# Contexts and organ weights turned outside the late stage, and 16 attention tiles turned by VectorE and a DMA round trip

## The chip, the cores and the metric

The kernel runs on one core of a Trainium2 chip. The metric is the device time of one execution in microseconds (us), lower is better. Every duration below comes from one profiled execution of the kernel before.

## What is computed

Two blocks of two layers each, on latents `x` of 16 batches x 64 tokens x 512 and a context `ctx_4096` of the same shape. Cut to what matters:

```python
x = x + L0_xattn(layernorm(x), ctx)      # 32 heads, 8 key/value heads, RMS-normed q and k, kv = [ctx, latents]
x = x + L0_ffn(layernorm(x))             # 4-bit weights (512 x 1376, twice, and 1376 x 512), silu(x Wg) * (x Wu) @ Wd
x = x + L1_xattn(ctx, layernorm(x), ctx) # below
x = x + L1_ffn(layernorm(x))             # x W_org^T + a mixture of 8 rank-64 products, weighted by softmax(mean(x) Wq^T keys^T)

def L1_xattn(k, q, v):                   # each (16, 64, 512); the 512 features are the positions
    scores = einsum('bcn,bcm->bnm', k, q) / sqrt(64)   # 512 x 512 in every batch
    return einsum('bnm,bcm->bcn', softmax(scores, axis=-1), v)
```

## The kernel before, in words

One program, all five engines, ordered by hand: each engine's instructions are written in the order in which it runs them, and semaphores join the engines. Products are made in a split form: a value is cut into a high part (rounded to fp32r, a `Copy` on ScalarE) and a low part (a subtraction on VectorE or GpSimd), and each 512-wide product is two or three matmuls of these parts.

The work comes in three stages:

- **L0 attention**, 64 steps (`run_steps`) of one key/value head and one pair of batches each. The context, turned so that features lie on partitions, stays in `kvT` for all of it. In every step the queries and the probabilities make a round trip through DRAM (`blocks_out`, `blocks_back`, tensors `q_turn` and `p_turn`): VectorE turns 32x32 blocks, one DMA writes them out and another reads them back in an order that finishes the turn of the tile. Beside it the 4-bit weights are unpacked in 35 chunks by `dequant` on VectorE and stored.
- **L0 FFN**, first half of the tokens, then the first three tiles of the second half (`pe_ffn` and its fellows).
- **The late stage** (`pe_slot`, `act_slot`, `dve_slot`, `pool_slot`), 64 *slots* and 8 more to run out. It holds L1 attention, the rest of the L0 FFN and the L1 FFN. Slot k begins with the scores of tile k (a batch has four tiles of 128 positions). What follows in the slots for one tile t: the row maximum (VectorE L1995), exp (ScalarE L1883, into `pr`), the scaling by 1/sum (GpSimd L2125), then the turn of the 128x512 tile by four TensorE transposes into a PSUM bank (`pe_weights`, L1588), its high part (ScalarE L1869) and low part (VectorE L1999) into `pmT`, and the two value products with the turned context `vS` (`pe_values`, L1604). In every slot up to 24 there are also 12 matmuls of the L0 FFN (`pe_piece`: `half_product` L1697 and `down` L1073). From slot 24 on the L1 FFN takes their place by a table `LATE` of (slot, half) to pieces: *base* (3 matmuls, L1715), *rank* (6, L1738), *delta* (3, L1748).

Tile t is turned in slot t + 5 (t + 6 from tile 24 on) and multiplied with the values in slot t + 6 (t + 8). *Extras* are groups of four TensorE transposes that stand between the two halves of a slot's work (`pe_extra`): the context of a pair of batches for `vS` (`pe_context`, L1513, followed by `act_values` and `dve_values`), the new latents x4, and in slots 17 to 21 and 23 the organ weights `W_org`, `Wq` and the keys (L1816, L1774, L1777). SP issues the DMAs of the late stage in a list of its own (`sp_l1x`): `stack` copies the high and low parts of a batch's context and queries (4 DMAs, L1422 and L1423), `context` loads `cx`.

Of the kernel before, what the change touches and what calls it, by code (L numbers as in the profile page):

```python
# [58 lines left out]
def block_kernel(nc, a, out, stop=None):  # L59
# [28 lines left out]
    with root:  # L88
# [104 lines left out]
        wq1 = at(185376, "wq1", [P, D], F32)  # L193
# [18 lines left out]
        keys = at(226784, "keys", [EXP, KD], F32)  # L212
# [668 lines left out]

        def sp_tables(sp, kinds):
# [48 lines left out]
        def sp_stores(sp, j):  # L931
# [145 lines left out]
        def pe_ffn(pe):  # L1077
# [3 lines left out]
            for n in range(FT + ALONE):  # L1081
# [11 lines left out]
                if n == FT + 1:  # L1093
                    pe_context(pe, 0)
# [24 lines left out]
        def x2_hi(act, p):  # L1119
            act.wait_ge(s_tx2, p + 1)  # L1120
# [12 lines left out]
        def act_ffn(act):  # L1133
            for n in range(FT + ALONE):
# [100 lines left out]
        def dve_ffn(dve):  # L1235
            for n in range(FT + ALONE):
# [23 lines left out]
                if n == FT + 1:  # L1260
                    dve_values(dve, 0)
# [31 lines left out]
        def add_down(dve, half):  # L1293
# [22 lines left out]
        (s_wot, s_woh, s_wol, s_sm, s_smc, s_dnh, s_dnl, s_uph, s_upl, s_tx4, s_x4h, s_x4l, s_mean) = (
            sem(f"s_{n}") for n in ("wot", "woh", "wol", "sm", "smc", "dnh", "dnl", "uph", "upl", "tx4", "x4h", "x4l", "mean"))
# [30 lines left out]
        def pr_of(n):  # L1348

            if n >= FAR // KT and n % 3 == 2:  # L1350
                return prw, 0
            return pr, KT * (n % 2 if n < FAR // KT else n % 3)

        def pm_of(t):
            return t % 2 if t < FAR else t % 3

        def x_bank(k):
            return bank[3] if k < WIDE else bank[6]

        def context_slot(q):  # L1360
            return PT_ * q - 2 if PT_ * q <= FAR else PT_ * q + 5

        def x4_slot(p):
            return sum_slot(2 * p + 1) + (2 if sum_slot(2 * p + 1) < WIDE else 3)
# [11 lines left out]
        def extra_evicted(pe, k):  # L1376

            kind, n = EXTRA[k]
            if kind == "context":
                pe.wait_ge(s_vTl, n + 1)  # L1380
            elif kind == "x4":
                pe.wait_ge(s_x4l, n + 1)
                pe.wait_ge(s_mean, n + 1)
            elif kind == "worg":
                pe.wait_ge(s_wol, n + 1)
            elif kind == "wq":
                pe.wait_ge(s_smc, 1)
            elif kind == "keys":
                pe.wait_ge(s_smc, 2)
# [835 lines left out]
```

## Time and profile before

| | |
|---|---|
| median of 3 runs | 1080.45 us (1080.32 to 1084.87) |
| the profiled execution | 1080.24 us, its span 1078.4 us |
| TensorE busy | 1038.6 us, 96% of the span |
| VectorE, ScalarE, GpSimd busy | 66%, 50%, 44% |
| mean granted TensorE clock | 0.995 |

The span runs from the first to the last instruction, and 1.84 us of the execution lie outside it. TensorE's busy share includes matmuls that overlap, so the length of a slot on TensorE, from one tile's scores to the next one's, is what prices are read from here.

### The profile page before, as it was taken

To read this page: it belongs to the slowest core of one execution; us is meant where nothing else is said; L and a number is where in the kernel's file an instruction comes from. 1 tells how busy PE (TensorE), PEld (TensorE's weight loads), DVE (VectorE), ACT (ScalarE), POOL (GpSimd) and SP (SyncE) were. 2 spreads that over 40 slices of the span, in tenths; PEclk is the share of its full clock that TensorE was granted. 3 is DMA by queue.
4 is the path that set the end of the run, shared out by engine and by line. 5 is a ranking of instruction groups with operands and counts; after the bars stand their busy time and mean duration, and the time that the engine had idled before them with its cause. 6 is when DMAs were issued, how large, how long until landed. Compare 5 with 4: busy or idle time off the path is not lost. (4 is left out here: it accounts for less than half of the span.)

```text
span 1078.4 us, 18680 instructions
## 1 busy us (share of the span) xinstructions
PE 1038.6 (96%) x6021; PEld 897.1 (83%) x6021; DVE 711.7 (66%) x1435; ACT 536.8 (50%) x1974; POOL 469.5 (44%) x446
## 2 busy tenths in 40 slices
PE   5899999999999999999999999899999999899998
PEld 5789999999899899899999998778777877677877
DVE  6677767667666667667676666653345666889862
ACT  3555555555555555555555454433324445456531
POOL 3445454565554554554645433300013325566521
PEclk9999999999999999999999999999999999899999
DMA  8447766676667666766666435242021344233301
GB/s 284 112 130 226 207 192 198 195 206 196 199 198 195 201 192 186 214 204 201 210 191 187 145 99 167 98 136 82 1 59 40 79 108 108 69 69 69 89 11 40
DMA packets 151397, 156.18 MB, mean 145 GB/s; under 512 B 19640, under 2 KB 104656, under 8 KB 151300
## 3 DMA queue, kind: packets, MB, share of 16 engines
q1 hardware_dynamic: 146804, 138.08, 44.0%
q0 software_dynamic: 4496, 16.91, 5.3%
q8 instruction: 49, 0.80, 0.3%
q14 instruction: 48, 0.39, 0.1%
HBM read 98.19 MB, written 44.30 MB: 132 GB/s over the span
## 5 line engine op out<-in xcount | busy, mean ns | idle before, releaser
L459 PEld LDWEIGHTS bank<-wqkv,kvT 128*128 128x128 f32 x1536 | 193.9, 193 | 8.2 <-issue 3.6
L439 PE MATMUL bank<-wqkv,kvT 128*128 128x512 f32 x768 | 195.4, 404 | 5.0 <-DVE wqkv L746 2.5
L459 PE MATMUL bank<-wqkv,kvT 128*128 128x256 f32 x1536 | 196.2, 285 | 3.0 <-issue 3.0
L800 POOL TENSOR_TENSOR rms<-msq,half_neg 128x4 f32<-128x4 f32 x64 | 79.5, 1242 | 270.0 <-DVE msq L703 270.0
L505 PE MATMUL bank<-wo,aoT 128*128 128x512 f32 x768 | 190.7, 398 | 0.3 <-DVE aoT L659 0.3
L439 PEld LDWEIGHTS bank<-wqkv,kvT 128*128 128x128 f32 x768 | 141.2, 191 | 34.1 <-issue 3.2
L505 PEld LDWEIGHTS bank<-wo,aoT 128*128 128x128 f32 x768 | 139.8, 189 | 26.4 <-DVE aoT L659 0.5
L606 ACT ACTIVATE prob<-bank,nmax 128x128 f32<-128x128 f32 x256 | 90.4, 365 | 56.4 <-DVE nmax L674 56.4
L646 ACT ACTIVATE aoT<-bank 128x512 fp32r<-128x512 f32 x64 | 38.2, 597 | 121.7 <-PE bank L526 96.2
L803 POOL TENSOR_TENSOR pT<-pR,pT 128x512 fp32r<-128x512 f32 x64 | 82.3, 1286 | 14.4 <-ACT pT L595 14.4
L613 ACT ACTIVATE qB<-bank 128x128 f32<-128x128 f32 x256 | 67.3, 278 | 39.7 <-PE bank L439 36.2
L711 DVE TENSOR_TENSOR bank<-bank,rms 128x512 f32<-128x512 f32 x64 | 44.8, 699 | 55.8 <-POOL rms L800 55.8
L1054 PE MATMUL bank<-x2T,wgu 128*128 128x512 f32 (+1 forms) x336 | 80.9, 396 | 0.4 <-DVE wgu L1015 0.4
L2125 POOL TENSOR_TENSOR pr<-pr,rc 128x512 f32<-128x512 f32 x52 | 54.4, 1048 | 54.5 <-DVE rc L1989 54.3
L674 DVE TENSOR_REDUCE nmax<-bank 128x4 f32<-128x512 f32 x64 | 44.2, 691 | 50.1 <-PE bank L469 50.0
L1054 PEld LDWEIGHTS bank<-x2T,wgu 128*128 128x128 f32 (+1 forms) x336 | 62.4, 187 | 15.9 <-DVE wgu L1015 0.8
L626 ACT ACTIVATE kT<-bank,wqk 128x256 f32<-128x256 f32 x64 | 30.6, 478 | 87.9 <-PE bank L485 87.9
L469 PE MATMUL bank<-kT,qT 128*128 128x128 f32 x512 | 67.8, 275 | 2.0 <-DMA qT<-q_turn 1.3
L1073 PE MATMUL bank<-wd,hT 128*128 128x512 f32 (+1 forms) x264 | 65.5, 396 | 0.0
L469 PEld LDWEIGHTS bank<-kT,qT 128*128 128x128 f32 x512 | 62.8, 192 | 2.5 <-DMA qT<-q_turn 1.5
L723 DVE TENSOR_TENSOR kn<-bank,rms 128x256 f32<-128x256 f32 x64 | 27.2, 425 | 52.0 <-POOL rms L808 52.0
L1869 ACT ACTIVATE pmT<-bank 128x512 fp32r<-128x512 f32 x64 | 38.2, 596 | 46.4 <-PE bank L1588 46.2
(176 smaller groups left out, 2021.4 us busy)
## 6 DMA issues: line engine op xcount, KB each, us to landing
q_turn<-qB SPq DMA_DIRECT2D x64, 256.0 KB
qT<-q_turn SPq DMA_DIRECT2D x64, 256.0 KB, 3.6
p_turn<-pB SPq DMA_DIRECT2D x64, 256.0 KB, 2.1
pR<-p_turn SPq DMA_DIRECT2D x64, 256.0 KB
qS<-qhl SPq DMA_DIRECT2D x32, 256.0 KB, 3.7
wqkv_raw<-in_L_xattn_Wq_dram SPq DMA_DIRECT2D x30, 256.0 KB
wo_raw<-in_L_xattn_Wo_dram SPq DMA_DIRECT2D x30, 256.0 KB
wload<-w_gu SPq DMA_DIRECT2D x20, 256.0 KB, 3.2
```

Of the source, the lines that this page charges most:

```text
L439: mm = pe.matmul(b_q[:, :], kvT[:, l, kt, p, 1:3, :], wqkv[:, par, r, kt, 0:QW], start=(kt == 0 and n == 0), stop=(kt == KT - 1 and n == 2))
L459: mm = pe.matmul(kv_bank(st, 0)[:, b * 256:(b + 1) * 256], kvT[:, l, kt, p, 2 * b:2 * b + 2, :], wqkv[:, par, r, kt, QW:QKV], start=(kt == ...
L469: mm = pe.matmul(b_s[:, n * P:(n + 1) * P], qT[:, n, :, :], kT[:, n // 2, :], start=True, stop=True)
L505: mm = pe.matmul(b_o[:, :], aoT[:, l, h, :, :], wo[:, par, r, h, :], start=(h == 0 and n == 0), stop=(h == G - 1 and n == 2))
L606: act.activation(prob[:, :, n, :], b_s[:, n * P:(n + 1) * P].rearrange("p (k b) -> p b k", b=4), ACT.Exp, bias=nmax[:, n:n + 1], accum_out ...
L613: act.activation(qB[:, h, :, :], b_q[:, h * HD:(h + 1) * HD], ACT.Square, accum_out=ssq[:, h:h + 1]).then_inc(s_qsq, 1)
L711: dve.tensor_tensor(b_n[:, :].rearrange("p (b h d) -> p b h d", b=4, h=G), b_q[:, :].rearrange("p (h d b) -> p b h d", h=G, b=4), rms[:, 0 ...
L800: pool.tensor_tensor(rms[:, 0:4], msq[:, 0:4], half_neg[:, 0:4], ALU.pow).then_inc(s_rq, 1)
L803: pool.tensor_tensor(pT[:, LO, :, :, :], pR[:, :, :, :], pT[:, HI, :, :, :].bitcast(F32), ALU.subtract).then_inc(s_plo, 1)
L1054: mm = pe.matmul(b[0:w, :], wgu[:, f, l, m, kt, 0:w], x2T[:, r, kt, :], start=(kt == 0 and k == 0), stop=(kt == KT - 1 and k == 2))
L1073: mm = pe.matmul(f_d[t][:, :], hT[0:w, l, t * P:(t + 1) * P], wd[0:w, f, r, :], start=(f == 0 and k == 0), stop=(f == FT - 1 and k == 2))
L2125: pool.tensor_tensor(of[:, to + t % KT, :], of[:, to + t % KT, :], rc1[:, t % 4:t % 4 + 1].to_broadcast([P, D]), ALU.mult).then_inc(s_n1, 1)
```

## The change

- **Contexts.** In steps 24 to 31 of L0 attention SP stores the turned contexts, high and low parts, from `kvT` to a DRAM tensor `ctx_turned` (`context_store`, four DMAs of 128 KB a step in runs of 256 bytes). In the late stage `vS` of a pair is one DMA load (`values`), and `pe_context`, `act_values` and `dve_values` are gone.
- **Organ weights and Wq.** In step 59 SP loads them into buffers of the unpacking, which has ended (`late_raw`), VectorE turns their 32x32 blocks in steps 60 to 62 (`late_turn`, five instructions), and SP stores them in steps 61 to 63 (`late_store`, 20 DMAs in runs of 128 bytes). In the late stage they are loaded already turned; their high parts are made on ScalarE from SBUF (`organ_hi`) and the low parts on GpSimd. The keys are loaded turned, by elements.
- **Tiles 0 to 15** (`TURN` = 16, four groups of four). exp writes its columns in another order; VectorE turns 32x32 blocks (`turn_tile`, 16 instructions), four DMAs write the group out (`turn_out`), four bring it back tile by tile (`turn_back`) into two landing places. The high part is taken in slot t + 7 from SBUF, the low part in the next slot, and the value products follow in slot t + 8. Tiles from 16 on are turned by TensorE in slot t + 7 up to tile 24 and t + 6 after that, all with values at t + 8.
- **The table LATE** is moved to fit: x4 of the first pairs comes 2 or 3 slots later, and so do the first rank pieces (from slot 34 instead of 32).

The core of the diff:

```diff
+        def context_store(sp, p):
+            sp.wait_ge(s_chi, PAIRS)
+            sp.wait_ge(s_clo, PAIRS - 1)
+            for to, (part, b) in enumerate(((HI, 0), (LO, 0), (LO, 1), (HI, 1))):
+                sp.dma_start(ctx_turned[p, :, :, to, :], kvT[:, part, :, p, 3 * b, :].bitcast(F32)).then_inc(s_ct_out, 16)
...
         def weights_slot(t):
-            return t + 5 if t < FAR else t + 6
+            return t + 7 if t <= FAR else t + 6
         def values_slot(t):
-            return t + 6 if t < FAR else t + 8
+            return t + 8
...
-        EXTRA = {**{context_slot(q): ("context", q) for q in range(1, PAIRS)},
-                 **{x4_slot(p): ("x4", p) for p in range(PAIRS - 1)},
-                 **{17 + i: ("worg", i) for i in range(KT)}, 21: ("wq", 0), 23: ("keys", 0)}
+        EXTRA = {x4_slot(p): p for p in range(PAIRS - 1)}
...
+            def turn_out(n):
+                sp.wait_ge(s_pB, UNITS + KT * (n + 1))
+                for m in range(KT):
+                    sp.dma_start(l_turn[n][m].rearrange("s u r -> (s u r)").rearrange("(p c) -> p c", p=P),
+                                 lB[:, m, :, :, :].rearrange("p b c j -> p (b c j)")).then_inc(s_p_out, 16)
+            def turn_back(t):
+                n, m = divmod(t, KT)
+                sp.wait_ge(s_p_out, outs(KT * (n + 1)))
+                if t >= 2:
+                    sp.wait_ge(s_p1l, t - 1)
+                sp.dma_start(lR[:, t % 2, :].rearrange("p (s r) -> p s r", s=G),
+                             l_turn[n][m].rearrange("s u r -> u s r")).then_inc(s_p_back2[t % 2], 16)
...
+            for n in range(B):
+                if n < TURN // KT:
+                    turn_out(n)
+                    turn_back(KT * n)
+                    turn_back(KT * n + 1)
+                    if n == 2:
+                        organ_loads()
+                    if n == 3:
+                        down_loads()
+                    turn_back(KT * n + 2)
...
+                if n + 3 < B:
+                    stack(n + 3)
...
+                if n < TURN // KT:
+                    turn_back(KT * n + 3)
...
         LATE = {
-            (24, 0): (("base", 0, 0),),
-            (25, 0): (("base", 0, 1),),
+            (24, 0): (("base", 0, 0), ("base", 0, 1)),
...
-            (32, 1): (("rank", 0, 0), ("rank", 0, 1),),
+            (34, 1): (("rank", 0, 0), ("rank", 0, 1),),
...
+            if k in TURNED_AT:
+                t = TURNED_AT[k]
+                act.wait_ge(s_p_back2[t % 2], backs(t))
+                if t >= 2:
+                    act.wait_ge(s_v1, t - 1)
+                act.activation(turned(HI, t), landed(t), ACT.Copy).then_inc(s_p1, 1)
...
+        def turn_tile(dve, t):
+            dve.wait_ge(s_n1, t + 1)
+            if t % KT == 0 and t >= KT:
+                dve.wait_ge(s_p_out, outs(t))
+            dve.transpose(lB[:, :, :, t % KT, :].rearrange("p m b j -> p (m b) j"),
+                          pr[:, t % KT, :].rearrange("p (k j) -> p k j", j=32)).then_inc(s_pB, 1)
```

**TensorE, slots 16 and 17.** Before (`ident` marks a transpose, `qS,kS` the scores that open a slot, `pmT,vS` the values that close it, `x2T,wgu` and `wd,hT` the FFN):

```order
L1568 MATMUL bank<-qS,kS 128x512 x2
L1588 MATMUL bank<-ident,pr 128x128 x4
L1073 MATMUL bank<-wd,hT 128x512 x6
L1822 MATMUL bank<-ident,xn 128x128 x4
L1073 MATMUL bank<-wd,hT 128x512 x6
L1604 MATMUL bank<-pmT,vS 128x512 x2
L1568 MATMUL bank<-qS,kS 128x512 x2
L1588 MATMUL bank<-ident,pr 128x128 x4
L1697 MATMUL bank<-x2T,wgu 128x512 x6
L1816 MATMUL bank<-ident,worg 128x128 x4
L1697 MATMUL bank<-x2T,wgu 128x512 x6
L1604 MATMUL bank<-pmT,vS 128x512 x2
```

The same two slots in the changed kernel:

```order
L1643 MATMUL bank<-qS,kS 128x512 x2
L1117 MATMUL bank<-wd,hT 128x512 x12
L1679 MATMUL bank<-pmT,vS 128x512 x2
L1643 MATMUL bank<-qS,kS 128x512 x2
L1771 MATMUL bank<-x2T,wgu 128x512 x12
L1679 MATMUL bank<-pmT,vS 128x512 x2
```

All 16 transposes of the two slots are gone (those of x4 stand in slot 19), and each run of 12 FFN matmuls is whole.

**VectorE, slots 15 and 16 of the changed kernel** (`nm` is the row maximum that opens a slot, `pmT<-pmT` the low part of a turned tile, `STREAM_TRANSPOSE` the block turn, `rc` the reciprocal of a row sum):

```order
L2058 TENSOR_REDUCE nm<-bank 128x1
L2062 TENSOR_TENSOR pmT<-pmT 128x4x4x32
L1334 TENSOR_TENSOR hT<-hval,hT 128x512
L2101 STREAM_TRANSPOSE pr<-pr 128x16x32 x2
L1320 SCALAR_TENSOR_TENSOR gact<-gact,bank 128x512
L2052 RECIPROCAL rc<-sm 128x1
L2058 TENSOR_REDUCE nm<-bank 128x1
L2062 TENSOR_TENSOR pmT<-pmT 128x4x4x32
L2122 TENSOR_TENSOR acc<-bank,acc 64x512
L2124 TENSOR_TENSOR acc<-bank,acc 64x512
L2101 STREAM_TRANSPOSE pr<-pr 128x16x32
```

Three block turns are new here, and the low part now reads its tile from SBUF instead of from a PSUM bank.

**SP, the third group (tiles 8 to 11) of the changed kernel:**

```order
L1483 DMA l_turn<-pr 128x512 x4
L1491 DMA pmT<-l_turn 128x4x128 x2
L1503 DMA worg<-organ_turned 128x4x512
L1491 DMA pmT<-l_turn 128x4x128
L1477 DMA kS<-chl 64x512
L1478 DMA qS<-qhl 64x1024
L1477 DMA kS<-chl 64x512
L1478 DMA qS<-qhl 64x1024
L1464 DMA vS<-ctx_turned 128x1024
L1491 DMA pmT<-l_turn 128x4x128
```

Before, SP's list held here only the stack, the context load and the loads of the organ weights; eight DMAs a group and one load of `vS` a pair are new.

## Rows read from the trace of the kernel before

**Rows 1.** The page, part 1: busy us (share of the span) xinstructions

```profile
PE 1038.6 (96%) x6021; PEld 897.1 (83%) x6021; DVE 711.7 (66%) x1435; ACT 536.8 (50%) x1974; POOL 469.5 (44%) x446
```

**Rows 2.** Windows of the late stage: slots 0-4, 5-7, 8-18, 19-24, 25-33, 34-41, rest

```profile
core 0: us, PE busy (x) PEld busy (x) DVE busy (x) ACT busy (x) POOL busy (x), PEclk, DMA share, GB/s
809.00:825.80 16.80, 16.43 (x71) 13.02 (x70) 9.05 (x19) 8.67 (x17) 6.89 (x8) 1.00 0.00 0
825.80:839.05 13.25, 13.04 (x63) 10.11 (x63) 6.93 (x14) 5.63 (x12) 4.62 (x5) 1.00 0.51 116
839.05:889.16 50.11, 49.21 (x238) 38.58 (x236) 33.97 (x65) 21.98 (x47) 14.96 (x17) 1.00 0.40 91
889.16:919.09 29.93, 29.45 (x146) 22.04 (x144) 19.18 (x38) 16.20 (x34) 15.22 (x14) 1.00 0.39 98
919.09:946.70 27.61, 22.64 (x117) 17.34 (x115) 22.66 (x49) 14.82 (x38) 16.67 (x18) 0.88 0.29 68
946.70:967.29 20.59, 19.29 (x113) 15.33 (x111) 17.95 (x39) 12.26 (x29) 14.68 (x17) 1.00 0.40 90
967.29:1078.40 111.11, 102.24 (x596) 84.27 (x596) 76.44 (x164) 45.89 (x111) 42.27 (x49) 1.00 0.20 51
```

**Rows 3.** Timeline of TensorE: starts of slots 2, 3, 8, 9, 17, 18, one value product

```profile
815.46 0.62 PE L1568 MATMUL bank<-qS,kS 128*128 128x512 f32 x2
...
818.71 0.63 PE L1568 MATMUL bank<-qS,kS 128*128 128x512 f32 x2
...
839.05 0.62 PE L1568 MATMUL bank<-qS,kS 128*128 128x512 f32 x2
...
842.75 0.63 PE L1604 MATMUL bank<-pmT,vS 128*128 128x512 f32 x2
843.22 0.63 PE L1568 MATMUL bank<-qS,kS 128*128 128x512 f32 x2
...
878.71 0.63 PE L1568 MATMUL bank<-qS,kS 128*128 128x512 f32 x2
...
883.58 0.64 PE L1568 MATMUL bank<-qS,kS 128*128 128x512 f32 x2
```

**Rows 4.** VectorE by source line: duration ns min/median/max

```profile
L696 DVE STREAM_TRANSPOSE pB<-bank x64: 716/716/717, 38.4 to 684.9; 128x512 f32<-128x512 f32 x64
...
L1288 DVE TENSOR_TENSOR hT<-hval,hT x22: 676/692/1043, 698.6 to 915.5; 128x512 fp32r<-128x512 f32 x20, 96x512 fp32r<-96x512 f32 x2
```

**Rows 5.** DMAs: SP's issue (ns), landing of the page's part 6 (us), of qT

```profile
L372 SPq DMA_DIRECT2D p_turn<-pB x64: 319/332/339, 39.2 to 685.7; - x64
...
L1423 SPq DMA_DIRECT2D qS<-qhl x31: 589/599/1900, 800.6 to 1008.0; - x31
...
p_turn<-pB SPq DMA_DIRECT2D x64, 256.0 KB, 2.1
...
draw<-in_L_ffn_lora_down_dram SPq DMA_DIRECT2D x4, 256.0 KB, 4.4
...
DMA to landing us min/median/max: 2.5/3.6/7.1
```

**Rows 6.** Timeline of L0 attention: pR issued, pR read; and the page's DMA slices

```profile
280.55 0.40 SPq L376 DMA_DIRECT2D pR<-p_turn  x1
...
287.24 0.65 ACT L595 ACTIVATE pT<-pR 128x512 fp32r<-128x512 f32 x1
...
DMA  8447766676667666766666435242021344233301
```

**Rows 7.** Timeline and window around slot 32: a wait, and TensorE's clock after it

```profile
937.49 1.22 PE L1568 MATMUL bank<-qS,kS 128*128 128x512 f32 x2 [2.38 <-DMA qS<-qhl]
...
939.67 2.90 PE L1738 MATMUL bank<-x4a,dn 128*128 128x256 f32 x12
...
948.08 1.57 PE L1738 MATMUL bank<-x4a,dn 128*128 128x256 f32 x12
...
937.00:941.00 4.00, 3.41 (x12) 2.75 (x13) 3.48 (x10) 2.33 (x6) 3.35 (x4) 0.50 0.96 244
```

More of the change, by code:

```diff
@@ L946, in sp_stores @@
                     weight_store(sp, c)
+            if CTX_AT <= j < CTX_AT + PAIRS:
+                context_store(sp, j - CTX_AT)
+            for i in range(LATE_TURNS):
+                if j == RAW_AT + 2 + i // 2:
+                    late_store(sp, i)
         def sp_loads(sp, j):
@@ L1223, in dve_ahead @@
             dve_between(dve, j, "end")
+            for i in range(LATE_TURNS):
+                if j == RAW_AT + 1 + i // 2:
+                    late_turn(dve, i)
             if j < 4:
@@ L1376, in extra_evicted @@
         def extra_evicted(pe, k):
[L1378 to L1389, printed above, removed]
+            pe.wait_ge(s_x4l, EXTRA[k] + 1)
+            pe.wait_ge(s_mean, EXTRA[k] + 1)
         SUMMED = {sum_slot(n): n for n in range(B)}
-        WEIGHTS_AT = {weights_slot(t): t for t in range(TILES)}
+        TURNED_AT = {weights_slot(t): t for t in range(TURN)}
+        WEIGHTS_AT = {}
+        for t in range(TURN, TILES):
+            WEIGHTS_AT.setdefault(weights_slot(t), []).append(t)
         VALUES_AT = {values_slot(t): t for t in range(TILES)}
@@ L1538, in pe_slot @@
                 pe_scores(pe, k)
-            if k in WEIGHTS_AT:
-                pe_weights(pe, k, WEIGHTS_AT[k])
+            for t in WEIGHTS_AT.get(k, ()):
+                pe_weights(pe, k, t)
             t = VALUES_AT.get(k)
-            last = t is not None and (t >= FAR and t % KT != 0 or k == FFN_END)
+            last = t is not None and t >= FAR and t % KT != 0
             if last:
@@ L1579, in pe_weights @@
                 pe.wait_ge(s_y2, PAIRS)
-            elif t >= 1:
+            elif t > TURN:
                 pe.wait_ge(s_p1l, t)
-            if t == 0:
-                pe.wait_ge(s_vTl, 1)
-            if k - 1 < WIDE and k - 1 in EXTRA:
+            if t == TURN:
+                extra_evicted(pe, max(j for j in EXTRA if j < k))
+            elif k - 1 <= FFN_END and k - 1 in EXTRA:
                 extra_evicted(pe, k - 1)
@@ L1995, in dve_slot @@
                 dve.tensor_reduce(nm1[:, t % 4:t % 4 + 1], s_bank(t)[:, :], AX, ALU.max, negate=True).then_inc(s_m1, 1)
-            if k in WEIGHTS_AT:
-                t = WEIGHTS_AT[k]
+            if k - 1 in TURNED_AT:
+                t = TURNED_AT[k - 1]
+                dve.wait_ge(s_p1, t + 1)
+                dve.tensor_tensor(turned(LO, t), landed(t), turned(HI, t).bitcast(F32), ALU.subtract).then_inc(s_p1l, 1)
+            for t in WEIGHTS_AT.get(k, ()):
                 dve.wait_ge(s_p1, t + 1)
@@ L2000, in dve_slot @@
                                   ALU.subtract).then_inc(s_p1l, 1)
+            if k % 3 == 0 and 3 <= k <= FFN_END:
+                hidden_lo(dve, FT + ALONE + k // 3 - 1)
             if k - 1 >= WIDE:
```

298 lines of the change are left out of this document (159 added, 139 removed).

## The prediction, as put on record

> **What bounds the kernel now.** I read the page's busy shares first: TensorE is busy for 96% of the span [rows 1], so time falls only where TensorE gets less to do or waits less. Then I cut the late stage, where the change acts, into windows at the starts of slots [rows 2]. The reader is to see two kinds. In slots 0 to 24 TensorE is busy in 16.43 of 16.80, 13.04 of 13.25, 49.21 of 50.11 and 29.45 of 29.93 us: it is the bound, and what is taken from it comes off the end. In slots 25 to 33 it works 22.64 of 27.61 us and VectorE 22.66: there the chain of VectorE sets the pace. From slot 34 on the two alternate (VectorE 76.44 and TensorE 102.24 of 111.11 us in the rest).
>
> **Prices.** Slot 2 holds scores and 12 FFN matmuls and lasts 818.71 - 815.46 = 3.25 us; slot 8 has a turned tile and a value product besides and lasts 843.22 - 839.05 = 4.17; slot 17 has an extra as well, 883.58 - 878.71 = 4.87 [rows 3]. The value product takes 843.22 - 842.75 = 0.47. So a turned tile costs TensorE 4.17 - 3.25 - 0.47 = **0.45 us**, and an extra that splits a run of FFN matmuls **0.70 us**, more than its four transposes.
>
> **Late stage, slots 0 to 24.** Slots 0 to 4 stay. Slots 5 to 7 lose three turned tiles, the context of pair 1 and, since values come eight steps behind, both value products: 3 x 3.25 = 9.75 us for 13.25, -3.5. Slots 8 to 18 become scores, 12 matmuls and values, 3.25 + 0.47 = 3.72 us each: 11 x 3.72 = 40.9 for 50.11, -9.2. Slot 19 has x4 (3.72 + 0.70 = 4.42), 20 to 22 are plain (11.16), 23 has a turned tile (4.17), and 24 two base pieces and a turned tile; its matmuls are 0.2 us more than before, and I give it 5.9. That is 25.65 for 29.93, -4.3. Together -17.0 us, if TensorE waits for nothing.
>
> **What could make it wait there.** The group path replaces four PSUM turns. The last of a group's block turns stands in slot 4n + 5 on VectorE and ends some 3.1 us into it, the first of its value products in slot 4n + 8 stands 3.25 us into it: 3 x 3.72 + 3.25 - 3.1 = 11.3 us of cover. The path: four issues at 0.33, a landing at 2.1 (four at once, so up to 1 more), an issue at 0.4, the way back as qT, 3.6 in the median [rows 5], the high part 0.65 (as pT [rows 6]), the low part 0.69 [rows 4]: 8.8 to 9.8 us. It fits with 1.5 us to spare, but ScalarE stands in a wait at the end of slot 4n + 7 for one or two us, and exp of the next tile is queued behind it; by the slot lengths I estimate that it has 1.5 us before the next scores need it. The other queue is SP's: `turn_back` of the third tile waits for a low part, and `stack` (0.6 us an issue, 1.9 at most [rows 5]), a 1 MB load and `vS` are queued behind it. All are due four slots on.
>
> VectorE gets 16 block turns of 0.72 us and loses the `vS` and organ low parts. Summing its instructions by slot at the durations of [rows 4], slots 8 to 18 hold some 36.5 us against TensorE's 40.9, but slots 15 to 18 hold 15.6 against 14.9, and `hval`, for which the FFN product of slot 18 waits, is the last of them. I charge **3 us** for all waits of slots 5 to 24 (bounds: 0, and 8 from the rivals below), leaving **-14.0**.
>
> **Slots 25 to 33.** VectorE's pace. It has 35 full-width instructions there instead of 30, and two half-width rank products (0.4 each) go: 5 x 0.69 - 0.8 = +2.6 us. Against that stands a loss of the profiled execution: at slot 32 TensorE waited 2.38 us for a stack, the granted clock then fell to 0.50, the 1.2 GHz level, and 12 rank matmuls took 2.90 us instead of 1.57 [rows 7]; slots 32 and 33 lasted 946.70 - 937.49 = 9.2 us for 6.0 of work, 3.2 lost. Now these two slots hold no rank piece, so a fall there costs little, but TensorE is less busy, and one may come in 34 and 35. I take **0** (bounds -3.2 + 2.6 = -0.6, and +3).
>
> **Slots 34 to 41.** The pieces moved back land here: two more ranks of 1.4 us and a base of 0.7, +3.5 us, into a stretch where TensorE is idle for 20.59 - 19.29 = 1.3 us [rows 2]. **+2.3** (bounds +1 and +3.5).
>
> **The rest.** Three contexts fewer, in slots 45, 53 and 61, and one in the FFN before slot 0: four groups at 0.44 (the transposes alone) to 0.70, **-2.0** (bounds -2.8, and -0.8 where VectorE is the bound). Their `vS` loads are due a pair ahead.
>
> **L0 attention.** In steps 24 to 31 SP issues four more DMAs, which at 0.33 to 0.6 us delay `q_out` and pR behind them by 1.3 to 2.4 us. pR is issued at 280.55 and read at 287.24 [rows 6]; with 3.6 us to land it has 3.1 us to spare. The five block turns follow the end of the unpacking and take its place on VectorE; their 20 small stores in steps 61 to 63 delay SP by up to 4 us once, and ScalarE has slack of its own after pT. **0** (bounds 0 and +3).
>
> **Sum.** -14.0 + 0 + 2.3 - 2.0 + 0 = -13.7 us, made against the profiled execution's own 1080.24: 1066.5. Its median neighbour is 0.2 us higher, which I ignore. A difference under about 0.5% (5.4 us) can't be told from none.
>
> A rule of the skill speaks against the stores. What the row shows: a 256 KB load in runs of 256 bytes lands in 4.4 us, a 256 KB store in long runs in 2.1 [rows 5], and DMA engines are 0.6 to 0.7 busy through L0 attention [rows 6]. The Trainium skill (DMA: Bandwidth & Descriptors, Specifications) says that a transfer needs runs of at least 512 bytes for line rate, since shorter ones are done by read-modify-write. No row of this case shows a store in runs of 256 bytes; by the rule alone the eight steps would lengthen, which is the third rival; by the row the sum stands.
>
> **Rivals.**
> 1. **VectorE becomes the bound of slots 8 to 24.** Its low parts now read both operands from SBUF; the one such form in the trace takes 0.69 us mostly and 1.04 at most [rows 4]. At 1.04 for 16 tiles, +5.6 us on an engine that is 90% full, and most of it shows. 1072. For: the sums above. Against: 21 of 22 are at 0.69.
> 2. **The round trip is late and the kernel is slower.** One mechanism: all four groups queue behind stacks and large loads. With issues like the worst of `qS` (1.9) and landings like the worst of qT, 7.1 us both ways [rows 5], the path is 1.9 + 1.0 + 7.1 + 0.4 + 7.1 + 1.3 = 18.8 us against 11.3 of cover: 7.5 late in each group, 30 in all, 1096. It decides from 3.4 us a group, 13.7 / 4. Against: the late stage's DMA share is 0.4 where L0 attention's is 0.7 with a median of 3.6 [rows 2, 6].
> 3. **The small stores fill the DMA engines in steps 24 to 31.** Worked out from rows: by the 4.4 us row, 512 KB a step is up to 8.8 us of a step of 10.3 (p_turn's 64 issues lie between 39.2 and 685.7 [rows 5]) that is 0.7 used; if half of that is engine time, the share is 1.13, 1.4 us a step, 11 in all: 1078. The skill's rule above would have this effect.
> 4. **The thin slots cost a slow clock.** If the clock falls in slots 34 and 35 as it did in 32 and 33, 3.2 us come back, and waits in 25 to 33 add 2: 1071.5.
>
> **How the numbers follow.** Chances: forecast 0.60, rival 1 0.17, rival 2 0.04, rival 3 0.04, rival 4 0.15. The low end is the sum with no waits in slots 5 to 24 and the best bounds of the other terms: 1080.2 - 17.0 - 0.6 + 1 - 2.8 = 1060.8; I take 1060.5. The high end holds rivals 1 and 4: 1074. Outside lie rivals 2 and 3 and some of both tails, under 0.2. Faster by over 0.5% is below 1075: 0.93; within, 0.04; slower, 0.03.
>
> **What the changed profile would show.** Slot lengths of 3.7 us in slots 8 to 18, where 4.2 to 4.9 stood; ScalarE waiting for the returned tile in slots 8, 12, 16 and 20 by one or two us and TensorE by little; VectorE near 90% there; slots 25 to 33 near 27 us and 34 to 41 near 23; L0 attention steps of 10.3 us as before. I am wrong if TensorE waits for scores or values once a group (rival 2), if steps 24 to 31 are longer than their neighbours (rival 3), or if the low parts take over 0.9 us (rival 1).

## The result, and the profile after

The changed kernel is slower: 1088.41 us (median of 8 runs, 1084.9 to 1095.12) against 1080.89 (8 runs, 1078.82 to 1084.87), ratio 1.0073 with a 95% interval of 1.0049 to 1.0097. The prediction was 1066.5, with 0.93 on faster.

The profiled execution of the changed kernel took 1095.12 us, its span 1093.3, the slowest of its eight runs and 6.7 us over their median, so the losses read from it are on the high side; that of before stands at its median. Its page, part 1 and the clock of part 2 (TensorE has 4 us less to do than in [rows 1], in a span 15 us longer):

```profile
PE 1034.7 (95%) x5904; PEld 891.4 (82%) x5904; DVE 724.3 (66%) x1444; ACT 530.4 (49%) x1964; POOL 476.7 (44%) x450
...
PEclk9999999999999999999999999899999999899999
```

**Late stage.** Windows of the changed kernel at the same slots as [rows 2] (slots 0-4, 5-7, 8-18, 19-24, 25-33, 34-41, rest), columns as there:

```profile
822.66:839.47 16.81, 16.44 (x72) 13.00 (x70) 10.88 (x22) 8.67 (x17) 6.90 (x8) 1.00 0.00 0
839.47:849.83 10.36, 9.98 (x44) 7.72 (x43) 6.08 (x11) 3.57 (x8) 3.58 (x4) 1.00 0.68 185
849.83:897.36 47.53, 42.33 (x178) 32.51 (x177) 39.24 (x71) 20.84 (x45) 18.41 (x19) 1.00 0.79 217
897.36:927.50 30.14, 27.18 (x115) 20.49 (x114) 20.35 (x37) 15.20 (x32) 19.50 (x17) 0.94 0.85 205
927.50:955.47 27.97, 21.36 (x99) 16.12 (x97) 20.83 (x43) 13.64 (x34) 13.80 (x14) 0.82 0.35 82
955.47:982.33 26.86, 23.17 (x137) 19.10 (x138) 23.15 (x50) 14.30 (x35) 18.16 (x20) 1.00 0.37 92
982.33:1093.30 110.97, 102.51 (x585) 83.92 (x584) 74.88 (x161) 44.12 (x108) 42.20 (x48) 0.98 0.23 60
```

Two things are to be seen. Slot 0 begins at 822.66 where it began at 809.00: 13.7 of the 14.9 us are lost before the stage that the change was read by. And in slots 8 to 18 TensorE does get 6.9 us less to do (42.33 for 49.21), but the windows shorten by 2.6 only; the DMA share there goes from 0.40 to 0.79. Slots 34 to 41 are 6.3 us longer.

**L0 attention.** Here I count steps from 0 by the unit whose scores open them on TensorE; SP issues for a step up to one ahead of that. In the kernel before every step from 6 to 61 lasts 10.20 us. Windows of the changed kernel: steps 23, 26, 27 and 30, then 60, 61 and 62:

```profile
270.94:281.14 10.20, 10.20 (x67) 9.21 (x65) 7.17 (x15) 5.55 (x25) 4.66 (x6) 1.00 0.96 241
...
302.36:313.53 11.17, 10.46 (x66) 9.13 (x65) 6.28 (x13) 5.65 (x25) 3.45 (x4) 1.00 0.87 232
313.53:326.16 12.63, 10.47 (x67) 9.13 (x66) 7.35 (x14) 5.44 (x25) 6.24 (x6) 1.00 0.82 227
...
348.14:359.96 11.82, 10.47 (x67) 9.14 (x66) 5.89 (x13) 5.65 (x25) 4.22 (x4) 1.00 0.77 207
...
655.80:666.42 10.62, 10.46 (x66) 9.12 (x65) 7.83 (x18) 4.92 (x24) 3.40 (x5) 1.00 0.64 148
666.42:679.42 13.00, 11.12 (x67) 9.49 (x66) 7.68 (x18) 5.95 (x26) 3.37 (x5) 0.96 0.72 189
679.42:692.75 13.33, 8.79 (x45) 7.81 (x45) 9.89 (x18) 5.31 (x16) 5.07 (x5) 0.76 0.49 151
```

The nine steps from 270.94 on take 99.22 us for 91.80, +7.4; the last three 36.95 for 30.42, +6.5. Up to step 6 this execution is 1.2 us ahead by chance, and 0.9 us more is lost between the last step and slot 0.

Why pR and qT are late is read in the timeline of SP's queue (start, duration of the issue). Before, then the changed kernel, one step each:

```profile
310.73 0.32 SPq L372 DMA_DIRECT2D q_turn<-qB  x1
311.15 0.38 SPq L376 DMA_DIRECT2D pR<-p_turn  x1
...
314.10 0.38 SPq L376 DMA_DIRECT2D qT<-q_turn  x1
```

```profile
311.80 2.59 SPq L894 DMA_DIRECT2D ctx_turned<-kvT  x4
314.50 0.59 SPq L370 DMA_DIRECT2D q_turn<-qB  x1
315.18 0.39 SPq L374 DMA_DIRECT2D pR<-p_turn  x1
...
321.13 0.37 SPq L374 DMA_DIRECT2D qT<-q_turn  x1
```

The four stores take 2.6 us of issue, and behind them `q_turn` needs 321.13 - 314.50 = 6.6 us until SP can issue `qT`, where it needed 3.4: the wait is for `q_turn` to land. What SP issues for the next step stands behind it in the same queue, so the delay adds up.

### The profile page after: what moved, and what is told of

Same layout as the page of the kernel before. It is cut to its first block and busy times, and to the rows that moved or that the text cites. A ratio compares the mean times of both kernels' runs of the same rounds, so it can differ in the third digit from the quotient of the medians.

```text
span 1093.3 us, 18540 instructions
## 1 busy us (share of the span) xinstructions
PE 1034.7 (95%) x5904; PEld 891.4 (82%) x5904; DVE 724.3 (66%) x1444; ACT 530.4 (49%) x1964; POOL 476.7 (44%) x450
## 5 line engine op out<-in xcount | busy, mean ns | idle before, releaser
L2193 POOL TENSOR_TENSOR pr<-pr,rc 128x512 f32<-128x512 f32 x48 | 52.1, 1086 | 48.6 <-DVE rc L2052 48.3
L524 PEld LDWEIGHTS bank<-pT,vv 128*128 128x128 f32 x384 | 54.3, 191 | 14.7 <-POOL pT L801 10.2
L524 PE MATMUL bank<-pT,vv 128*128 128x256 f32 x384 | 57.2, 286 | 7.7 <-POOL pT L801 7.7
```

Of the source, the lines that this page charges most:

```text
L524: mm = pe.matmul(b_pv[:, b * 256:(b + 1) * 256], vv[:, par, l, b, :], pT[:, r, :, b, :], start=(n == 0), stop=(n == 2))
L2193: pool.tensor_tensor(of[:, to + t % KT, :], of[:, to + t % KT, :], rc1[:, t % 4:t % 4 + 1].to_broadcast([P, D]), ALU.mult).then_inc(s_n1, 1)
```

## The experiments

Each run has its median, the ratio to before measured beside it, and its interval. The runs were measured in four groups, each with its own runs of before (medians 1079.76 to 1081.05 us), so runs of different groups are compared by their ratios. Lengths of stretches come from its profiled execution. *Slots 12-24* is from the start of slot 12 to that of slot 25.

**e1_spread: the context stores, one a step.**

```diff
-            if CTX_AT <= j < CTX_AT + PAIRS:
-                context_store(sp, j - CTX_AT)
+            if CTX_AT <= j < CTX_AT + 4 * PAIRS:
+                context_store(sp, *divmod(j - CTX_AT, 4))
```

> The same 32 context stores, one in each of steps 24 to 55 instead of four in each of steps 24 to 31. Theory A (four stores a step fill the DMA engines, 0.86 busy where 0.64 stood, and pR comes back late): at one a step the share rises by 0.06 only, every step from 24 to 55 lasts 10.20 us again, and the 7.4 us lost in steps 25 to 31 come back: about 1081. Rival B (each store costs by standing in SP's queue, 0.65 us of issue, wherever it is): the loss is only spread, 0.2 us a step, and the time stays near 1088.

1086.46 us, 1.0043 (1.0029 to 1.0057). The window of the nine steps from 24 on:

```profile
283.78:375.58 91.80, 91.80 (x578) 82.86 (x577) 62.91 (x127) 51.08 (x225) 49.19 (x43) 1.00 0.73 212
```

Nothing is lost there, in this and the seven later runs with one store a step; the six profiled executions with four a step lost 3.9 to 8.0 us. That the crowding of four stores in a step is the cause is shown, its price less sharply: the ratio fell by 0.0030, 3.2 us of the 7 expected, with an uncertainty of 0.0028. Whether the DMA engines or SP's 2.6 us of issue do more is not told apart, since the spreading relieves both.

**e2_five: the organ weights by five plain stores.** `late_store` is one DMA a tile, and the late stage loads the blocks in their turned order.

```diff
-            for k in range(KT):
-                sp.dma_start(to[:, 32 * k:32 * (k + 1)].rearrange("(b r) c -> r b c", r=32), ...)
+            sp.dma_start(to, spare[i - 1]).then_inc(s_late_out, 16)
...
+                for b in range(KT):
+                    sp.dma_start(worg[32 * b:32 * (b + 1), :, :].rearrange("r t (x c) -> r t x c", c=32), blocks[b])
```

> The organ weights and Wq are stored as five plain tiles in runs of 2 KB, and the order of the blocks is made by the late loads (four DMAs each for Wq and W_org, runs of 128 bytes); 15 issues go from steps 61 to 63, six more stand in slots 12 and 16. Theory A (the 20 issues of about 0.55 us hold q_turn, qT and pR back on SP, and the gap they cause in steps 61 to 64 is followed by half the clock): steps 60 to 64 give back most of the 6.6 us they lost, up to 8 with the half clock: 1080 to 1083. Rival B (the five raw loads, the five block turns on VectorE or the wait for the stores before the FFN are what costs): less than 2 us come back. The late stage may lose 1 to 2 us to the smaller runs of the loads.

1089.55 us, 1.0073 (1.0054 to 1.0091): no gain. Step 61 loses 0.2 us instead of 2.8, so the 20 scattered stores were its cause (their issue time or their short runs, which the edit changes together); step 62 still loses 2.8 with 6.8 us at half the clock, and slots 16 to 19 take 21.2 us for 18.5: the four blockwise loads of `worg` take 6.2 us to issue, and ScalarE waits 3.4 us for them. What was saved was paid elsewhere.

**e3_values_after: vS of pair 2 behind the fourth group's first returns.**

```diff
                     turn_back(KT * n + 1)
+                    if n == 3:
+                        values(2)
...
-                if n % 2 == 0 and n >= 2 and (n + 2) // 2 < PAIRS:
+                if n % 2 == 0 and n >= 4 and (n + 2) // 2 < PAIRS:
```

> The 1 MB load of vS for pair 2 is issued after the fourth group's stores and its first two returns instead of before them. Theory A (the group's stores of 1 MB land late, 8.2 us after the first issue, because the vS load issued 3 us before shares the DMA engines): the fourth group's stores land 2 to 4 us sooner, ScalarE's waits in slots 19 and 20 shrink, slots 18 to 21 lose 2 to 3 us of their 20.9: about 1086. Rival B (VectorE's stretched instructions set these slots): no change in slots 18 to 21.

1093.09 us, 1.0121 (1.0102 to 1.014), slower than the changed kernel; its profiled execution was the fastest of its runs. There slots 18 to 21 took 17.5 us for 20.9, so theory A holds where it was made: the fourth group's first return is issued 7.6 us after its first store instead of 9.6. But slots 22 and 23 took 11.2 us for 8.0, with TensorE waiting 1.6 us for a low part in slot 22, and slots 16 to 24 together are 0.3 us shorter. Why the median rose was not settled. (The load of `vS` is 512 KB, not the 1 MB of the expectation.)

**e4_thin: the other transfers of the late stage, thin.**

```diff
+                n = P if q < 2 else 4
+                sp.dma_start(cx[0:n, q % 2, :], ctx_t[q][0:n])
...
+                    if n >= 2:
+                        to = slice(part * T, part * T + 4)
+                        rows = slice(b * T, b * T + 4)
```

> Left out of the computation: most of the contents of the late stage's stacks from batch 2 on, of cx and of vS from pair 2 on (each DMA moves 4 partitions instead of 64 or 128; its issue and its semaphore stay). Theory A (the round trip of the four groups is late because these transfers share the DMA engines, 0.83 busy in slots 12 to 18): landings of the groups' stores fall from 4.3 to 9 us to under 3, ScalarE no longer waits 3.45 us for the tile in slot 12, slots 8 to 24 take 70 us or less for 77.7, and the time falls by 6 to 10 us: 1078 to 1082. Rival B (VectorE is the bound, with its low parts at up to 1.55 us beside GpSimd): slots 8 to 24 keep over 75 us and the stretched instructions.

1089.08 us, 1.0061 (1.0039 to 1.0083). Slots 12-24 took 59.2 us instead of 62.7, against 51.7 in the prediction's sum (7 x 3.72 + 25.65), and slots 8 to 24 took 74.2 us, between the two theories. What ScalarE waited for from slot 8 to slot 24, in the changed kernel and in e4 (us in total, times, longest):

```profile
ACT pmT L1964 <- DMA pmT<-l_turn: 16.0, 9, 3.5
ACT pr L1942 <- DVE nm L2058: 14.0, 9, 3.5
```

```profile
ACT pr L1947 <- DVE nm L2063: 17.9, 14, 3.7
ACT pmT L1969 <- DMA pmT<-l_turn: 1.2, 1, 1.2
```

The waits for the returned tile fell from 16.0 to 1.2 us: `l_turn`'s stores now land in 3.2 us in the median and 3.8 at most, where the changed kernel has 3.9 and 8.1. Yet only 3.5 us came back. Behind the round trip stands VectorE, busy for nearly all of slots 16 to 19, with low parts of 1.17 us in the mean:

```profile
885.03:903.45 18.42, 15.95 (x69) 12.18 (x68) 17.95 (x31) 9.85 (x22) 8.76 (x9) 1.00 0.51 171
```

**e6_low_short and e7_both_thin: a smaller low part, alone and with e4.**

```diff
+                if t < 2:
+                    dve.tensor_tensor(turned(LO, t), landed(t), turned(HI, t).bitcast(F32), ALU.subtract)
+                else:
+                    dve.tensor_tensor(pmT[:, pm_of(t), LO, 0:32], lR[:, t % 2, 0:32], ...)
```

> Left out of the computation: all but 32 columns of the low parts of turned tiles 2 to 15; the transfers are whole. It completes a square with the changed kernel (slots 12 to 24: 62.7 us), e4 (thin transfers: 59.2) and e7 (both: 56.0). Theory A (VectorE's low parts and the landings each limit in other slots and add up): slots 12 to 24 take 59 to 60 us, some 3 less. Rival B (only the landings count as long as they are late): over 61.5 us.

> Left out of the computation: what e4 leaves out, and all but 32 columns of the low parts of turned tiles 2 to 15. e4 alone took slots 12 to 24 from 62.7 to 59.2 us, and the plain sum of the prediction gives about 51. Theory A (the landings and VectorE's stretched low parts each hide behind the other): with both taken off slots 12 to 24 fall to 52 to 55 us. Rival B (VectorE's other instructions and their order alone bound these slots): they stay above 57 us.

e6: 1088.71 us, 1.0079 (1.0062 to 1.0095); e7: 1086.06, 1.0047 (1.0027 to 1.0067). Slots 12-24: 62.7 (changed), 61.1 (e6), 59.2 (e4), 56.0 (e7). The two edits give 1.5 and 3.5 us alone and 6.6 together. e6's 61.1 and e7's 56.0 both lie between their two theories: some of the low part's cost hides behind the landings, and the other way round. 4.3 us over the sum's 51.7 remain even then, and no run tells what makes them.

**e5_low_pool: the low parts on GpSimd**, with e1's stores.

```diff
-                dve.tensor_tensor(turned(LO, t), landed(t), turned(HI, t).bitcast(F32), ALU.subtract)
+                pool.tensor_tensor(turned(LO, t), landed(t), turned(HI, t).bitcast(F32), ALU.subtract)
```

> With the context stores spread as in e1, the 16 low parts of the turned tiles are made by GpSimd (1.28 us each) instead of VectorE. Theory A (VectorE is the bound of slots 12 to 24: its busy time is 17.8 of 18.5 us in slots 16 to 19, with low parts stretched to 1.2 to 1.5 us beside GpSimd): slots 12 to 24 lose 3 to 5 us of their 62.9 (e1), 1082 to 1083. Rival B (the landing of the round trip is the bound, and the low part only follows it): no change or up to 2 us longer, since GpSimd's low part takes 0.6 us more and scales the next tile behind it.

1093.74 us, 1.0124 (1.0103 to 1.0144), 0.8% or 9 us over e1 by the ratios. Slots 8 to 19 took 57.3 us for 51.3, and in them TensorE waited 8.4 us for GpSimd's low parts, where in e1 it waited for no low part. Rival B, and more than it allowed: the work taken from VectorE, the fuller engine, went to the one that the value products then waited for.

**e12_turn_first: block turns ahead of the low part**, with e1's stores.

```diff
+            if k >= 2 and (k - 2) % KT >= 2 and k - 2 < TURN:
+                turn_tile(dve, k - 2)
             if k - 1 in TURNED_AT:
```

> With the context stores spread as in e1, the block turns of the third and fourth tile of a group stand right behind the row maximum in their slot, before the low part of a returned tile, instead of at the slot's end. Theory A (each group's round trip starts some 2 us sooner, and the low part no longer meets GpSimd's scaling, which starts 0.7 us before it and makes it wait): the low parts take 0.7 us in most slots, ScalarE's waits in slots 12, 16 and 20 shrink by 1 to 2 us each, slots 12 to 24 take 3 to 5 us less than the 62.9 of e1: 1082 to 1083. Rival B (VectorE's sum alone sets the pace, its order does not): under 1 us.

1087.12 us, 1.0064 (1.0044 to 1.0084). Slots 12-24 took 60.9 us for 62.9, 2 us of the 3 to 5. ScalarE's waits for the tile fell from 13.4 to 12.6 us only, so the earlier start gave little; the twelve low parts of that stretch took 0.81 us in the mean for 0.95, which is 1.6 us. Of theory A's two reasons the second holds. The median does not show the gain: the ratio is 1.0064 for e1's 1.0043.

**e8_no_late: no organ part in steps 59 to 63**, with e1's stores. `late_raw`, `late_turn` and `late_store` are not called, so the late stage works with weights that were not turned, and

```diff
-                sp.dma_start(worg[:, :, :], organ_turned.rearrange("(t p) o -> p t o", p=P))
+                sp.dma_start(worg[:, :, :], a["L1_ffn_W_org"].rearrange("(t p) o -> p t o", p=P))
```

> With the context stores spread as in e1, the loads, block turns and stores of the organ weights and Wq in steps 59 to 63 are left out; the late stage loads the weights unturned, the same bytes from the inputs. It prices that part by itself. Theory A (the 20 issues and the gap they make in steps 60 to 63 cost 6.4 us there and 0.9 before slot 0, half of it as half clock): steps 60 to 63 lose nothing against 10.2 us a step, slot 0 comes 7 us sooner than in e1, 1079 to 1081. Rival B (the last steps lose their time to something else, such as the wait for the context stores or the FFN's weight loads): less than 3 us come back.

1077.62 us, 0.9981 (0.9969 to 0.9992), 0.62% or 6.7 us under e1 by the ratios. The window of the last three steps, in e8 and in e1:

```profile
649.96:680.70 30.74, 27.35 (x175) 24.22 (x174) 22.38 (x48) 16.46 (x66) 11.73 (x12) 1.00 0.44 142
```

```profile
650.99:688.99 38.00, 30.48 (x174) 26.11 (x173) 25.35 (x52) 16.22 (x66) 11.88 (x13) 0.91 0.60 159
```

Theory A: 7.3 us there, and 1.5 more before slot 0, in two profiled executions of which e1's is the slowest of its seven.

**e9_ctx_alone: the kernel before, with the contexts alone** (stores as in e1, `values` loads, no `pe_context`).

```diff
-        EXTRA = {**{context_slot(q): ("context", q) for q in range(1, PAIRS)},
-                 **{x4_slot(p): ("x4", p) for p in range(PAIRS - 1)},
+        EXTRA = {**{x4_slot(p): ("x4", p) for p in range(PAIRS - 1)},
...
+                if q >= 2:
+                    values(q)
                 stack(2 * q + 1)
```

> The kernel before, with one part of the change alone: contexts stored in steps 24 to 55, one DMA a step, and vS loaded in the late stage; the eight groups of context transposes are gone. Theory A (in slots 0 to 24 TensorE is the bound, and an extra costs 0.70 us there): slots 5 to 7, 8 to 15 and 16 to 24 each lose 0.7 us, the later ones 1 to 2 together, nothing is lost in L0 attention: 1077 to 1079. Rival B (the 1 MB loads of vS meet the stacks, and stacks come late as in slot 32 of before): the stacks' landings grow over 5 us, TensorE waits for scores, and the time stays at 1080 or over.

1076.43 us, 0.9961 (0.9945 to 0.9976), faster than before. Slots 5 to 15 took 46.6 us for 48.1, and slots 16 to 24 44.9 for 45.2 (0.3 us for the 0.7 expected); one stack came late, by 2.0 us, as one does in before (2.38 [rows 7]).

**e10_five_after and e11_ctx_organ: the organ stores in step 64.** e10 is e1 with e2's five stores moved behind the last query; e11 is e9 with that organ part, so that tiles are turned by TensorE as before.

```diff
+            if j == UNITS:
+                for i in range(LATE_TURNS):
+                    late_store(sp, i)
```

> With the context stores spread as in e1 and the organ weights as five plain stores and blockwise loads as in e2, but the five stores are issued in step 64, when no more queries follow. Raw loads and block turns stay in steps 59 to 62. Theory A (what costs in steps 60 to 63 is any large late DMA ahead of the queries' and probabilities' round trips; e8 without them lost nothing): steps 60 to 63 lose under 1 us for 7.4 (e1), no half clock stands near 680 us, 1078 to 1080. Rival B (the raw loads of 1.25 MB or the five block turns on VectorE cost as much as the stores): 3 us or more remain and the clock still falls.

> The kernel before with the contexts as in e9 and the organ part as in e10; tiles are turned by TensorE and the table is that of before. Theory A (slots 17 to 23 are TensorE's, and each of six extras costs 0.5 to 0.7 us there): slots 16 to 24 take 41 us for 44.9 in e9, L0 attention loses under 1 us, 1072 to 1074. Rival B (GpSimd's low parts of the organ weights, the late clock or a longer last step take it back): 1076 or over.

e10: 1083.26 us, 1.0031 (1.0018 to 1.0044), 0.12% under e1, which can't be told from none. Steps 60 to 62 lose 2.0 us for 7.4, between the two theories, and the clock still falls for 3.4 us; slots 16 to 19 take 21.3 us for 18.4, as in e2 with the same blockwise loads of `worg`. e11: 1073.61 us, 0.9934 (0.992 to 0.9949): **faster than both kernels**, by 0.7% than before and 1.4% than the change, and its slots 16 to 24 took the 40.4 us that theory A gave as 41. These two differ by the turned tiles, the lag of eight steps and the table, 9.7 us. Windows of slots 8-15, 16-24, 25-33 and 34-41, e11 then e10:

```profile
841.43:875.67 34.24, 34.03 (x161) 27.00 (x160) 22.60 (x43) 14.56 (x32) 11.17 (x12) 1.00 0.38 64
875.67:916.05 40.38, 39.95 (x192) 30.95 (x191) 28.23 (x53) 21.44 (x45) 24.36 (x23) 1.00 0.76 156
916.05:942.04 25.99, 21.35 (x117) 16.19 (x115) 22.85 (x49) 14.94 (x38) 16.16 (x17) 0.93 0.39 92
942.04:961.54 19.50, 18.59 (x109) 14.98 (x107) 17.21 (x38) 11.76 (x28) 15.08 (x18) 1.00 0.44 104
```

```profile
837.27:869.83 32.56, 30.61 (x130) 23.74 (x129) 25.27 (x45) 14.69 (x32) 12.41 (x12) 1.00 0.70 195
869.83:917.39 47.56, 40.43 (x163) 30.40 (x162) 35.07 (x61) 21.32 (x45) 25.51 (x24) 0.93 0.96 210
917.39:944.21 26.82, 20.03 (x98) 14.98 (x96) 20.78 (x43) 13.75 (x34) 13.84 (x14) 0.87 0.37 89
944.21:971.03 26.82, 23.09 (x137) 19.02 (x138) 23.11 (x50) 14.30 (x35) 18.14 (x20) 1.00 0.37 89
```

Turned tiles gain 1.7 us in slots 8 to 15 and 2.0 in slots 5 to 7; they lose 7.2 in 16 to 24, where the DMA share is 0.96, and 7.3 in 34 to 41, of which the slots from 42 on give 1.8 back.

**e13_table: e11 with the changed table LATE.**

```diff
-            (32, 1): (("rank", 0, 0), ("rank", 0, 1),),
...
+            (34, 1): (("rank", 0, 0), ("rank", 0, 1),),
...
```

> e11 with the changed kernel's table LATE and nothing else of its late stage: rank pieces from slot 34 on, values six steps behind up to tile 23 as before. Theory A (slots 34 to 41 last as long as VectorE's work in them, and most of what came there is the values', layer norms' and x4's work that the lag of eight moved, not the ranks): slots 34 to 41 grow by 1 to 2.5 us over e11's 19.5, slots 25 to 33 shrink by as much, the time stays within 1 us of e11. Rival B (the table alone makes the 26.8 us of slots 34 to 41): 25 us or more there, and 1077 or over.

1074.01 us, 0.9943 (0.993 to 0.9955), as e11. Slots 34 to 41 took 24.5 us, slots 25 to 33 22.8:

```profile
913.50:936.30 22.80, 16.71 (x86) 12.12 (x85) 20.87 (x45) 12.96 (x33) 13.17 (x15) 0.93 0.41 97
936.30:960.76 24.46, 22.67 (x137) 18.55 (x135) 19.70 (x43) 13.66 (x33) 18.41 (x21) 1.00 0.42 97
```

Neither theory had the size: the table alone moves 5 us to slots 34 to 41, but slots 25 to 33 and those from 42 on give them back. Of these 5 us TensorE's own work is 4.1 (22.67 for 18.59) and VectorE's 2.5 (19.70 for 17.21). The other 2.4 us of the change's 26.9 go with what else the change does there; that the lag of eight is most of it was not tried alone.

## Why the prediction was wrong, by its steps

| Term | predicted | profiled executions | 
|---|---|---|
| slots 5-7 | -3.5 | -2.9 |
| slots 8-18 | -9.2 | -2.6 |
| slots 19-24 | -4.3 | +0.2 |
| waits charged for slots 5-24 | +3 | in the rows above |
| slots 25-33 | 0 | +0.4 |
| slots 34-41 | +2.3 | +6.3 |
| rest | -2.0 | -0.1 |
| L0 attention, context stores | 0 | +7.4 |
| L0 attention, organ stores, and up to slot 0 | 0 | +7.4 |
| start-up (chance) | - | -1.2 |
| sum | -13.7 | +14.9 |

**L0 attention: "0 (bounds 0 and +3)" failed**, and with it the sign; two sentences of it did. "With 3.6 us to land it has 3.1 us to spare" sets one delay of SP against one spare stretch. In steps 23 to 31 the loads back land no later than before (3.1 us in the median for 4.2); what is late is their issue. The four stores ahead of `q_turn` take 2.6 us of SP, `q_turn` itself then needs 6.6 us for 3.4, and what one step issues late starts the next one late. Neither of the last two stood in the sum. This was the place and the sign of rival 3 (11 us, 0.04): 7.4 here and 3.9 to 8.0 in six executions. Its mechanism, full DMA engines, is not told apart from SP's issue time: the share rose from 0.69 to 0.84 in the nine steps, not to 1.13.

The rule of the Trainium skill behind it (DMA: Bandwidth & Descriptors, Specifications: runs under 512 bytes miss line rate and are done by read-modify-write) the trace bears out in direction. In its packet records of that stretch a packet of 256 bytes takes 19 ns in the mean and one of 512 bytes 29, so short runs cost 1.3 times the time for their bytes; whether by a read-modify-write it does not show.

The second sentence, "their 20 small stores ... delay SP by up to 4 us once": they delay it by 5.6 us in one step (663.05 to 668.62), and this was called covered because ScalarE "has slack of its own". SP and TensorE in step 61, changed kernel:

```profile
662.66 0.34 SPq L370 DMA_DIRECT2D p_turn<-pB  x1
663.05 2.12 SPq L915 DMA_DIRECT2D organ_turned<-qch  x4
665.21 3.41 SPq L915 DMA_DIRECT2D organ_turned<-rows  x4
...
670.26 0.38 SPq L370 DMA_DIRECT2D q_turn<-qB  x1
670.73 0.38 SPq L374 DMA_DIRECT2D pR<-p_turn  x1
...
678.17 1.45 PE L524 MATMUL bank<-pT,vv 128*128 128x256 f32 x6 [1.88 <-POOL pT L801]
```

`pR` is issued at 670.73 behind eight stores and three weight loads, TensorE waits 1.88 us for its low part, and the six matmuls behind the wait take 1.45 us instead of 0.88, at 1.2 GHz. e8 shows the price of the organ part here, 0.62% or 6.7 us. With the 0.30% of the crowded context stores that is 10 us by the ratios. Without both the kernel stands at 0.9981 (e8), 2 us under before where the prediction had 13.7: the sign was lost in L0 attention, and some 12 us more in the late stage.

**Slots 5 to 24: the waits were charged 3 us and took 11.7** (17.0 less the 5.3 gained). The path was costed right (the trip fits when the queues are quiet: slots 8 to 11 took 15.0 us, 4 x 3.72 = 14.9), its landings were not. `l_turn`'s stores land in 3.9 us in the median and 8.1 at most, not 2.1 to 3.1, and e4 shows that the stacks, `cx` and `vS` beside them are the reason for the late ones. SP, fourth group:

```profile
891.88 2.09 SPq L1483 DMA_DIRECT2D l_turn<-pr  x4
901.43 0.92 SPq L1491 DMA_DIRECT2D pmT<-l_turn  x2
```

9.55 us from the first store to the first return: the prediction had 1.3 + 3.1. The other groups take 5.5, 5.9 and 6.8. That is rival 2's mechanism at less than its size: slots 8, 12, 16 and 20, in which the first tile of a group gets its low part and its value product, are 0, 3.2, 1.2 and 2.6 us over 3.72, under the decision point of 3.4 a group. The wait reaches TensorE by a way that the prediction did not have. Slot 12:

```profile
866.74 0.64 ACT L1964 ACTIVATE pmT<-pmT 128x512 fp32r<-128x512 f32 x1 [3.45 <-DMA pmT<-l_turn]
...
867.41 0.69 DVE L2062 TENSOR_TENSOR pmT<-pmT 128x512 fp32r<-128x512 f32 x1 [1.00 <-ACT pmT L1964]
...
870.43 0.69 DVE L2124 TENSOR_TENSOR acc<-bank,acc 64x512 f32<-64x512 f32 x1
...
871.18 0.73 PE L1679 MATMUL bank<-pmT,vS 128*128 128x512 f32 x2 [2.33 <-DVE acc L2124]
```

The value product waits 2.33 us, not for its own tile, but for `acc`, VectorE's addition of the batch before, which stands behind the late low part in VectorE's order. Slot 20 has the same wait, 2.0 us. "Against: the late stage's DMA share is 0.4" used the share of the kernel before, to which the change itself adds 0.4.

Rival 1 was true as well: low parts took 0.93 us in the mean, not 0.69, and shortening them gives 1.5 us alone (e6) and 3.2 on top of e4 (e7). That both hold together was not weighed. e7 still leaves 5.2 of the 11.7 us (17.0 less the 11.8 that its slots 5 to 24 gain on before), which stay open.

**Slots 25 to 33: right by luck.** The 0 was taken from +2.6 for five more full-width instructions on VectorE and -3.2 for the clock. The first did not come: VectorE is busy for 20.83 us with 43 instructions, where [rows 2] has 22.66 with 49. The second was lost again (rival 4 below). Where the clock stayed up, in e8, the nine slots took 23.8 us, far under the low bound of 27.0.

**Slots 34 to 41: idle time was taken as room.** I set two ranks and a base, 3.5 us of TensorE, against its idle 1.3 us. TensorE got 3.9 us more (23.17 for 19.29), and its idle time did not shrink but grew to 3.7. VectorE, busy for 17.95 of the 20.59 us in [rows 2], gets 11 more instructions, 23.15 us in a window of 26.86; these were not priced. The window is 26.8 to 26.9 in all eleven profiled executions with turned tiles, whatever else was changed. Which engine sets its pace is not shown: in e13, with the table alone, VectorE gets only 2.5 us more and 5 us are lost all the same.

**Rival 4** came true in slot 28 instead of 34 and 35: TensorE waited 2.69 us for a low part, the granted clock was then 0.50 for 10.2 us, and slot 28 took 8.1 us for 3.0 of before. Over the execution the mean clock fell from 0.995 to 0.986, which is 31 us of span at half rate for 10; it cost at most half of the difference, 10 us.

**Right** were the price of slots 8 to 11 and the -3.5 of slots 5 to 7 within 0.6. The parts by the ratios to before: contexts -0.39% (e9), organ part with its stores in step 64 -0.27% (e11 less e9), turned tiles with lag and table +0.97% (e10 less e11), organ stores in steps 61 to 63 instead +0.12% (e1 less e10), context stores in eight steps instead of 32 +0.30% (changed kernel less e1), each uncertain by 0.16 to 0.28%, so that the last but one can't be told from none and the last barely; together +0.73%.

## What to carry to other kernels

A stage that a change only passes through has to be costed like the one it aims at: here 32 and 20 DMAs beside other work, priced at nothing, cost some 10 us against a predicted gain of 13.7, because an in-order queue carried a round trip with 3 us to spare and a delay in one step is handed to the next. Take landings and DMA shares for a new round trip from the busiest window that it will stand in, its own bytes added, and never from a median of quiet ones. Price moved work by what every engine gets in the window where it lands, and don't take idle time there as room to be filled; and when a change has several parts, time each alone, since two of the three here were gains.

## What the runs showed of the hardware

**VectorE waits for GpSimd when both its operands lie in SBUF.** VectorE, then GpSimd, in slots 17 and 18 of the changed kernel:

```profile
889.07 0.69 DVE L2058 TENSOR_REDUCE nm<-bank 128x1 f32<-128x512 f32 x1
889.68 1.55 DVE L2062 TENSOR_TENSOR pmT<-pmT 128x512 fp32r<-128x512 f32 x1
891.15 0.70 DVE L2101 STREAM_TRANSPOSE pr<-pr 128x512 f32<-128x512 f32 x1
...
895.91 1.52 DVE L1334 TENSOR_TENSOR hT<-hval,hT 128x512 fp32r<-128x512 f32 x1
```

```profile
889.64 1.04 POOL L2193 TENSOR_TENSOR pr<-pr,rc 128x512 f32<-128x512 f32 x1
...
895.40 1.49 POOL L2193 TENSOR_TENSOR pr<-pr,rc 128x512 f32<-128x512 f32 x1
```

The low part that starts at 889.68 ends 0.55 us after GpSimd's instruction, which ends at 890.68; the one at 895.91 is an `hT` low part and ends 0.54 after 896.89. Alone each takes 0.69. It is no shared rate but a turn taken: in e7 a low part of 32 columns takes 0.18 us alone and up to 1.15 beside GpSimd. `nm` and the other instructions that read a PSUM bank keep their 0.69, and so does the block turn, which has one input in SBUF (all 16 between 0.66 and 0.71). GpSimd waits too: its scaling at 895.40 takes 1.49 instead of 1.04. The Trainium skill says this (SBUF — State Buffer, SBUF: two separate sides): the pair of ports is an exclusive lock that a VectorE instruction with two SBUF inputs and a GpSimd one hold for its whole length. The trace agrees with it. The scaling starts with the reciprocal. Of the 16 low parts seven start less than 1 us behind it, and an eighth meets another GpSimd instruction; these took 0.79 to 1.55 us, the other eight 0.68 or 0.69.

**Half the clock is hard to price.** Around the last steps of L0 attention it fell in every profiled execution with an organ part (3.4 to 10.2 us long), once in e9, and in neither e8 nor before; after the waits of slots 25 to 33 it fell in all but e8, for 3.4 to 10.2 us. The changed kernel's eight runs differ by 10 us, those of before by 6.
